# Attention over 32 small graphs on one core: the softmax shares spread by POOL and turned by PE, eight heads' weighted sums in one block, twelve places for turned tiles, one bank for values and output

## The reference

```python
q, k, v = (proj(Wq, bq), proj(Wk, bk), proj(Wv, bv))      # (b, 8, 256, 32) each
scores = jnp.einsum('bhqd,bhkd->bhqk', q, k) * SCALE       # SCALE = 32 ** -0.5
scores = scores * (adj + adj)[:, None, :, :]
attn = jax.nn.softmax(scores, axis=-1)
ctx = jnp.einsum('bhqk,bhkd->bhqd', attn, v)               # heads side by side: (b, 256, 256)
out = jnp.einsum('bse,fe->bsf', ctx, Wo) + bo
y = x + out
result = (y - mean(y)) / sqrt(var(y) + 1e-5)               # over the features
```

## Time and profile before

| | |
|---|---|
| median of three runs | 520.39 us (519.92 to 523.06) |
| the profiled execution, its own time | 522.89 us |
| its span, first to last instruction | 521.1 us |
| mean granted clock of TensorE | 0.974 of full |

### The profile page before, as it was taken

The page is one execution under the profiler, slowest core; times in us unless marked ns, Lnnn a source line. Parts: engine busy times, 40 slices in busy tenths (PEclk is TensorE's granted clock), DMA queues, the critical chain, the costliest instruction groups (busy, mean ns, idle before and its releaser), DMA issues.

```text
span 521.1 us, 15227 instructions
## 1 busy us (share of the span) xinstructions
PE 472.7 (91%) x4742; PEld 395.2 (76%) x4742; DVE 429.8 (82%) x1815; ACT 384.0 (74%) x1257; POOL 348.7 (67%) x518
## 2 busy tenths in 40 slices
PE   4569999999999999999999999999999999998872
PEld 3357887878788788878888787878888787877752
DVE  4547888888888898888888998988889888888881
ACT  2478887777878777787878777787878777777750
POOL 4724557686876767696876767786776768664444
PEclk9859999999999999999999999999999999999996
DMA  5709897988889798898889897998989889795101
GB/s 161 173 29 240 207 222 176 233 202 205 227 208 240 173 254 193 218 219 206 227 202 235 199 244 173 230 219 205 231 187 260 187 220 214 165 246 128 61 23 41
DMA packets 40322, 100.11 MB, mean 192 GB/s; under 512 B 9649, under 2 KB 17842, under 8 KB 40242
## 3 DMA queue, kind: packets, MB, share of 16 engines
q1 hardware_dynamic: 26930, 73.96, 60.8%
q10 hardware_dynamic: 13312, 25.17, 16.8%
HBM read 26.22 MB, written 8.39 MB: 66 GB/s over the span
## 4 chain that ended last, share of the span: by engine, by line
PE 65%; POOL 21%; issue 5%; DVE 4%; ACT 3%; DMA 1%; POOLq 0%; DVEq 0%; SPq 0%; ACTq 0%
PE turn_bank L223 17%; PE proj_bank L240 11%; PE v_bank L253 9%; PE row_bank L211 8%; PE ctx_bank L278 8%; POOL xt_parts L546 7%; PE ctx_bank L266 5%; PE out_bank L290 5%; POOL parts L540 4%; POOL result L586 3%; POOL ctx_parts L554 2%; POOL scale L573 2%; POOL parts L538 2%; ACT probs L447 2%; POOL ctx_parts L552 1%
## 5 line engine op out<-in xcount | busy, mean ns | idle before, releaser
L447 ACT ACTIVATE probs<-probs,low_top 128x256 f32<-128x256 f32 x512 | 257.6, 505 | 100.9 <-DVE low_top L349 98.4
L356 DVE COPY turned_probs<-turn_bank 128x512 f32<-128x512 f32 x224 | 154.7, 691 | 53.7 <-PE turn_bank L223 52.9
L341 DVE CUSTOM_DVE_ANT_0 probs<-row_bank,adj_rows 128x256 f32<-128x256 f32 x512 | 192.2, 414 | 6.1 <-PE row_bank L211 6.1
L223 PE MATMUL turn_bank<-ident,probs 128*128 128x128 f32 x1024 | 158.2, 277 | 7.8 <-ACT probs L447 7.7
L223 PEld LDWEIGHTS turn_bank<-ident,probs 128*128 128x128 f32 x1024 | 119.5, 141 | 52.1 <-ACT probs L447 23.4
L240 PE MATMUL proj_bank<-xt_parts,w_parts 128*128 128x512 f32 x360 | 107.0, 407 | 21.4 <-POOL xt_parts L546 16.2
L211 PE MATMUL row_bank<-stack 128*128 128x256 f32 x512 | 124.3, 325 | 0.7 <-DVE top L341 0.7
L447 ACT ACTIVATION_READ_ACCUMULATOR probs<-probs,low_top 128x1 f32 x512 | 97.3, 190 | 0.0
L540 POOL TENSOR_TENSOR parts<-whole,parts 128x512 fp32r<-128x512 f32 x64 | 82.9, 1296 | 5.3
L240 PEld LDWEIGHTS proj_bank<-xt_parts,w_parts 128*128 128x128 f32 x360 | 61.0, 193 | 30.8 <-POOL xt_parts L546 19.2
L552 POOL CAST ctx_parts<-context 128x256 fp32r<-128x256 f32 x64 | 25.5, 398 | 86.0 <-DVE context L366 86.0
(11 more groups left out here) (44 smaller groups left out, 473.0 us busy)
## 6 DMA issues: line engine op xcount, KB each, us to landing
stack<-parts SPq DMA_DIRECT2D x492, 128.0 KB, 2.6
xt<-in_x_t SPq DMA_DIRECT2D x16, 512.0 KB, 3.9
adj_rows<-in_adj ACTq DMA_DIRECT2D x16, 512.0 KB, 4.7
xr<-in_x ACTq DMA_DIRECT2D x16, 512.0 KB, 7.5
out<-result ACTq DMA_DIRECT2D x32, 256.0 KB, 3.2
turned_probs<-in_wk SPq DMA_DIRECT2D x1, 256.0 KB, 4.0
turned_probs<-in_wq SPq DMA_DIRECT2D x1, 256.0 KB, 3.8
turned_probs<-in_wv SPq DMA_DIRECT2D x1, 256.0 KB, 4.0
```

What stands on the lines that cost most here:

```text
L223: last = nc.tensor.transpose(turn_bank[o % 2][:, c * S + t * P:c * S + (t + 1) * P], probs[:, o % RING, t * S + c * P:t * S + (c + 1) * P] ...
L341: last = nc.vector.tensor_tensor_reduce(probs[:, o % RING, t * S:(t + 1) * S], row_bank[o % 2][:, t * S:(t + 1) * S], adj_rows[:, (n // 2) ...
L356: nc.vector.tensor_copy(turned_probs[:, o, :], turn_bank[o % 2][:]).then_inc(moved_dve, 1)
L447: last = nc.scalar.activation(tile, tile, ACT.Exp, bias=low_top[:, n % 2, o, t:t + 1], accum_out=sums[:, n % 2, o, t:t + 1])
```

## The change

The two halves of a graph are joined. DVE divides once for eight heads, at head 7 of step g, and `sums` and `shares` are laid out with the node tile outside and the head inside. A new instruction on POOL, `spread_shares`, at head 7 of step g, ahead of whatever else stands there and behind `add_bias`, copies the 16 shares of a partition, each repeated 32 times, into `wide` (128x512). PE's `turn_shares` is then four plain 128x128 transposes of `wide` into a bank of their own, `inv_bank`; it waits for POOL's copy. It and `weigh_v`, now 32 matmuls for eight heads into the whole of `ctx_bank`, stand at head 1 of step g+1; at head 5 nothing is left. ACT's `copy_inverse`, DVE's `scale_context` and POOL's `cut_context` handle 512 columns once in a graph, at heads 2, 3 and 3 of step g+1. `turned_probs` has 12 places used in turn in place of 8. To free the bank for `inv_bank`, values and output share one: `project_v` also waits until the residual of the graph two back has been read from it, `project_out` until ACT has copied the values of graph g+2. The two uses of the bank stand where they stood.

```diff
+TURNED = 12
...
-        sums = sb("sums", [P, 2, H, T])
-        shares = sb("shares", [P, 2, H, T])
+        sums = sb("sums", [P, 2, T, H])
+        shares = sb("shares", [P, 2, T, H])
         probs = sb("probs", [P, RING, T * S])
-        turned_probs = sb("turned_probs", [P, H, T * S])
-        inverse = sb("inverse", [P, S])
-        context = sb("context", [P, 2, S])
+        turned_probs = sb("turned_probs", [P, TURNED, T * S])
+        wide = sb("wide", [P, T, H, D])
+        inverse = sb("inverse", [P, 2 * S])
+        context = sb("context", [P, 2 * S])
...
-        w_whole = turned_probs[:, 4:8, :].rearrange("p w (t e) -> p w t e", t=T)
+        w_whole = turned_probs[:, 8:12, :].rearrange("p w (t e) -> p w t e", t=T)
...
+        inv_bank = bank("inv_bank")
...
-        v_bank = bank("v_bank")
+        v_bank = out_bank
...
             def project_v(n):
                 if n == 0:
                     pe.wait_ge(w_cut, 3)
+                    pe.wait_ge(bias_ready, 1)
+                wait(pe, y_ready, n - 2)
                 wait(pe, v_ready, n)
...
-            def turn_shares(g, half_):
-                pe.wait_ge(shares_ready, 2 * g + half_ + 1)
-                wait(pe, ctx_ready, 2 * g + half_)
-                for t in range(T):
-                    for o in range(J * half_, J * half_ + J):
-                        c = D * (o % J)
-                        nc.tensor.matmul(ctx_bank[c:c + D, S + t * P:S + (t + 1) * P],
-                                         shares[:, g % 2, o, t:t + 1].to_broadcast([P, D]), ident[:], start=True, stop=True,
-                                         tile_position=(0, c), skip_group_check=True)
-            def weigh_v(g, half_):
-                if half_ == 0:
-                    pe.wait_ge(v_ready, g + 1)
-                for o in (J * half_ + J - 1, *(n for n in ON_ACT if n // J == half_)):
+            def turn_shares(g):
+                pe.wait_ge(widened, g + 1)
+                wait(pe, inverted, g)
+                for half_ in range(2):
+                    for t in range(T):
+                        last = nc.tensor.transpose(inv_bank[:, half_ * S + t * P:half_ * S + (t + 1) * P],
+                                                   wide[:, t].rearrange("p h d -> p (h d)")[:, half_ * P:(half_ + 1) * P],
+                                                   ident[:])
+                last.then_inc(inv_made, 1)
+            def weigh_v(g):
+                pe.wait_ge(v_ready, g + 1)
+                wait(pe, ctx_ready, g)
+                for o in (H - 1, *ON_ACT):
                     wait_moved(pe, g, o)
-                for t in range(T):
-                    for o in range(J * half_, J * half_ + J):
-                        c = D * (o % J)
-                        last = nc.tensor.matmul(ctx_bank[c:c + D, 0:S], v[:, (g // 2) % 2, g % 2, t, o * D:(o + 1) * D],
-                                                turned_probs[:, o, t * S:(t + 1) * S], start=(t == 0), stop=(t == T - 1),
-                                                tile_position=(0, c), skip_group_check=True)
+                for half_ in range(2):
...
+                        for o in range(J * half_, J * half_ + J):
...
                 last.then_inc(ctx_made, 1)
...
             def project_out(g):
-                pe.wait_ge(ctx_low, 2 * g + 2)
-                wait(pe, y_ready, g)
+                pe.wait_ge(ctx_low, g + 1)
+                pe.wait_ge(v_ready, min(g + 3, B))
...
                     if o == 1 and is_graph(g - 1):
-                        turn_shares(g - 1, 1)
-                        weigh_v(g - 1, 1)
+                        turn_shares(g - 1)
+                        weigh_v(g - 1)
                     if o == 2 and is_graph(g + 1):
                         project_v(g + 1)
-                    if o == 5 and is_graph(g):
-                        turn_shares(g, 0)
-                        weigh_v(g, 0)
                     if o == 6 and is_graph(g - 1):
                         project_out(g - 1)
...
             def move_turned(g, o):
...
-                wait(dve, ctx_made, 2 * g - 1 + o // J)
-                nc.vector.tensor_copy(turned_probs[:, o, :], turn_bank[o % 2][:]).then_inc(moved_dve, 1)
-            def divide(g, half_):
-                dve.wait_ge(probs_ready, 8 * g + J * half_ + J)
-                heads = slice(J * half_, J * half_ + J)
-                nc.vector.reciprocal(shares[:, g % 2, heads, :], sums[:, g % 2, heads, :]).then_inc(shares_ready, 1)
-            def scale_context(g, half_):
-                dve.wait_ge(inverted, 2 * g + half_ + 1)
-                wait(dve, ctx_low, 2 * g + half_ - 1)
-                nc.vector.tensor_tensor(context[:, half_, :], ctx_bank[:, 0:S], inverse[:],
-                                        ALU.mult).then_inc(ctx_ready, 1)
+                wait(dve, ctx_made, (H * g + o - TURNED) // H + 1)
+                nc.vector.tensor_copy(turned_probs[:, (H * g + o) % TURNED, :], turn_bank[o % 2][:]).then_inc(moved_dve, 1)
+            def divide(g):
+                dve.wait_ge(probs_ready, H * g + H)
+                wait(dve, widened, g - 1)
+                nc.vector.reciprocal(shares[:, g % 2], sums[:, g % 2]).then_inc(shares_ready, 1)
+            def scale_context(g):
+                dve.wait_ge(ctx_made, g + 1)
+                dve.wait_ge(inverted, g + 1)
+                wait(dve, ctx_low, g)
+                nc.vector.tensor_tensor(context[:], ctx_bank[:], inverse[:], ALU.mult).then_inc(ctx_ready, 1)
...
-                        divide(g - 1, 1)
+                    if o == 7 and is_graph(g):
+                        divide(g)
...
                     if o == 3 and is_graph(g - 1):
-                        scale_context(g - 1, 1)
-                    if o == 4 and is_graph(g):
-                        divide(g, 0)
-                    if o == 6 and is_graph(g):
-                        scale_context(g, 0)
+                        scale_context(g - 1)
...
-                                                accum_out=sums[:, n % 2, o, t:t + 1])
...
             def move_turned(g, o):
...
-                wait(act, ctx_made, 2 * g - 1 + o // J)
-                if g == 0:
-                    act.wait_ge(bias_ready, 1)
-                nc.scalar.copy(turned_probs[:, o, :], turn_bank[o % 2][:]).then_inc(moved_act, 1)
-            def copy_inverse(g, half_):
-                act.wait_ge(ctx_made, 2 * g + half_ + 1)
-                wait(act, ctx_ready, 2 * g + half_)
-                nc.scalar.copy(inverse[:], ctx_bank[:, S:2 * S]).then_inc(inverted, 1)
+                wait(act, ctx_made, (H * g + o - TURNED) // H + 1)
+                nc.scalar.copy(turned_probs[:, (H * g + o) % TURNED, :], turn_bank[o % 2][:]).then_inc(moved_act, 1)
+            def copy_inverse(g):
+                act.wait_ge(inv_made, g + 1)
+                wait(act, ctx_ready, g)
+                nc.scalar.copy(inverse[:], inv_bank[:]).then_inc(inverted, 1)
...
                     if o == 2 and is_graph(g - 1):
-                        copy_inverse(g - 1, 1)
+                        copy_inverse(g - 1)
...
-                    if o == 6 and is_graph(g):
-                        copy_inverse(g, 0)
...
-            def cut_context(g, half_):
-                pool.wait_ge(ctx_ready, 2 * g + half_ + 1)
+            def spread_shares(g):
+                pool.wait_ge(shares_ready, g + 1)
+                wait(pool, inv_made, g)
+                nc.gpsimd.tensor_copy(wide[:].rearrange("p t h d -> p (t h) d"),
+                                      shares[:, g % 2].rearrange("p t h -> p (t h)").unsqueeze(2).to_broadcast([P, T * H, D])
+                                      ).then_inc(widened, 1)
+            def cut_context(g):
+                high, low = (ctx_parts[:, g % 2, n].rearrange("p f s -> p (f s)") for n in range(2))
+                pool.wait_ge(ctx_ready, g + 1)
                 wait(pool, out_made, g - 1)
-                nc.gpsimd.tensor_copy(ctx_parts[:, g % 2, 0, half_, :], context[:, half_, :]).then_inc(ctx_high, 1)
-                pool.wait_ge(ctx_high, 2 * g + half_ + 1)
-                nc.gpsimd.tensor_tensor(ctx_parts[:, g % 2, 1, half_, :], context[:, half_, :],
-                                        ctx_parts[:, g % 2, 0, half_, :].bitcast(F32), ALU.subtract).then_inc(ctx_low, 1)
+                nc.gpsimd.tensor_copy(high, context[:]).then_inc(ctx_high, 1)
+                pool.wait_ge(ctx_high, g + 1)
+                nc.gpsimd.tensor_tensor(low, context[:], high.bitcast(F32), ALU.subtract).then_inc(ctx_low, 1)
...
                 for o in range(H):
+                    if o == 7 and is_graph(g):
+                        spread_shares(g)
...
                     if o == 3 and is_graph(g - 1):
-                        cut_context(g - 1, 1)
+                        cut_context(g - 1)
...
                     if o == 6 and is_graph(g):
                         add_bias(g // 2, g % 2)
```

(23 more changed lines are left out.)

## The result

The changed kernel takes 583.47 us in the median of four runs (581.64 to 584.28), against 520.76 for the kernel before: a ratio of 1.120 (95% interval 1.118 to 1.122). The forecast was 571, 553 to 591, slower. The profiled execution took 581.64, with a span of 579.8 us; the other three took 583.45 to 584.28.

What follows compares the result with a forecast made beforehand. Not PE's 91% but a loop through DVE's context and POOL's queue was taken to bound the kernel. Longer pairs (+42.5) with start and end made +44, span 565; clock falls +7 made 572, or 571 as time; range 553 to 591.

Steps and rivals of the forecast that it cites:

- the loop: PE's head 3, DVE's context, POOL's queue, back to PE: sets the step; a pair 32.84 against 29.57 us.
- Odd: Odd step, head 3 to head 3: 2.05 to POOL's start, 8.55 POOL queue, 4.57 PE, 15.17 us in all.
- Even: Even step, head 3 to head 3: the odd step's sum plus two low_x on POOL, 2.50, making 17.67 us.
- PE's wait at low x: In even steps PE stands about 2.6 us until POOL has the low part of x ready.
- The spread: POOL's new 128x512 repeated-read copy: taken at 0.69 us with its wait, ends 0.40 and 1.30.
- The clock: PE's clock falls after the long wait in half of 13 even steps, 1.1 us each: +7, ends 0 and +20.
- Rival 1: PE's clock stays warm, all else as forecast: 564 us; chance 0.27.
- Rival 2: Spread dear (1.30 us) or PE cold in each even step: 578 to 590 us; chance 0.22.
- rival 3: PE is the bound and POOL's lag is made up, PE giving back 23.0 us: about 499; chance 0.06.
- Rival 4: Spread never late, only the even step's wait for low x grows: 521 to 545 us; chance 0.07.
- some 0.6 more: Odd steps: added PE time where heads 4 to 6 come faster than DVE and ACT make them, 0.6 us.
- places and bank: Twelve places for turned tiles and the bank shared by values and output: cost nothing.

Runs made afterwards that it cites:

- experiment 6: Changed kernel with DVE's scale_context and POOL's cut_context at head 2 in place of head 3: 528.02 us, ratio 1.013.
- experiment 10: Kernel before with only scale_context and cut_context of the second half at head 2 in place of head 3: 509.88 us, ratio 0.977.
- experiment 3: Changed kernel with 8 unread matmuls of 512 columns on PE just ahead of the wait for low x: 576.67 us, ratio 1.105.
- experiment 4: Changed kernel with 20 transposes of the identity on PE filling the wait for low x: 572.79 us.
- experiment 1: Changed kernel with POOL's spread moved ahead of add_bias: 555.44 us, ratio 1.066.
- experiment 7: Changed kernel with the context at head 2 and the spread ahead of add_bias: 526.49 us, ratio 1.009.
- experiment 11: Changed kernel with context at head 2, spread ahead of add_bias, and some key/query matmuls moved from head 4 to head 5: 513.09 us, ratio 0.985.
- experiment 5: Kernel before with only twelve places for turned tiles and one bank for values and output: 521.12 us, ratio 1.0005.
- experiment 2: Changed kernel with POOL's spread made twice, the extra copy into a spare tile: 589.96 us.
- experiment 9: Changed kernel without POOL's spread, PE laying the shares out as before with 32 matmuls on 32-column strips: 582.91 us.

## Why the prediction was right, and where it was off

- **What bounds the kernel.** Right. Not the 91% but the loop: the context's one-head shift (experiments 6 and 10) moved the time by 54 and 12 us with no work removed.
- **The sum of the steps.** Odd: 15.17 forecast, 15.24 measured. Even, clock at full speed: 17.67 forecast, 17.63 measured. PE's wait at low x was put at 2.6 and is 2.3; the wait for the spread at 1.0 and 0.4, measured 0.88 and, warm, 0.17 (in a cold step none). Thirteen pairs at full clock would be 42.9 above those of before, against 42.5. Outside the pairs the forecast had +2, for steps 0, 1 and 28, and nothing for all behind them. Measured is +2.1, in other places: nothing up to step 2's head 3, and all of it in the last steps, where the span ends 66.6 behind step 28's head 3 (513.23) and ended 64.5 before (456.61).
- **The spread.** Taken at 0.69 with its wait, measured 0.61 long and 0.62 from start to start: no dearer than the cast, the repeated read costs nothing.
- **The clock: the term that was mis-sized.** "A fall in half of the 13 even steps at 1.1: +7." Measured: a fall in 11 of 13 at 1.22, that is 13.4. The mechanism was right (experiments 3 and 4), its count was a guess between ends and came out near the far one. This is 6.4 of the 7.8 by which the span of 579.8 exceeds the 572 of the forecast. Of the other 1.4, 0.7 lies in the pairs (0.4 in their warm length, the rest in cold steps that are a little longer than 18.85) and the remainder is rounding. The ground "waits of 1.06 leave it at 1.00" holds for the rows that it names, but not in general: in experiment 3 the clock was at 0.50 behind waits of 1.05 and 0.96.
- **From the profiled run to the median.** The profiled execution is the fastest of the four, 1.8 under their median, while the profiled one of before was 2.5 above the median of three to which the forecast was scaled. The distance of 12.5 from 571 is thus 6.4 clock, 1.4 other terms and 4.7 the runs' scatter, to which the count of falls belongs.
- **Rival 1** (warm) had 564, a span of 565: by the pairs of experiment 3 the span would have been 566.8 here. **Rival 2** gave 578 to 590 and is what happened in its second form, the falls in nearly each even step. It had a chance of 0.22 where the forecast had 0.38. That the measured time still lies between 553 and 591 is owed to the far end of that range, which is this rival's, and not to the count of falls that the forecast took. **Rivals 3 and 4** are out: POOL's queue to the spread takes the 8.5 of its rows (295.37 to 303.89 in the odd step). Rival 4's sum is right for the case that it names, the spread ahead of add_bias: experiment 1 built it, and its pair is 17.24 + 14.15 where the sum has 17.23 + 14.17. But the ground on which rival 3 stood, PE's saving, holds in no version: it goes into waits for exponentials (experiments 7 and 11), which the prediction counted only as "some 0.6 more".
- **Nothing for places and bank**: right, by experiment 5.
- The Trainium skill (TensorE: Matmul & The Clock Gate, HAM oscillation) has a kernel go cold at every wait of its loop. The waits of that kernel were longer than the 2.3 here, and this trace does not quite follow it: the clock fell in 11 pairs of 13, and in 4 of 13 with the same wait in experiments 1 and 2. For the changed kernel the rule was nearer than the half I took; for those two it was further off.

What stays open: why a wait of 2.3 drops the clock in one pair and not in the next. Within one run it repeats: eleven times in a row here, every second or third pair in experiment 1, every third up to step 21 in experiment 2. The length of the pair alone does not settle it, as a pair is 32.9 warm and 34.1 cold here, 31.4 warm in experiment 1 and 34.0 warm in experiment 2. The place of the wait in time may matter; no run here varied that alone.

## What to carry to other kernels

Before taking work from the busiest engine, follow the last wait of a step around: if it closes a loop through another engine's queue, what counts is what that queue does between its late start and the instruction waited for. The average shares of both engines said nothing of it here. When halves are merged, each instruction gets cheaper per element, but the first result comes later and the longer instruction delays all that is queued behind it; look for a place where the consumer can take it one slot sooner, which here was worth 54 us and cost nothing. Leave work in each slot of the engine that feeds the others (experiment 11).

## What the runs showed of the hardware

- POOL's 128x512 copy with each of 16 values read 32 times took 0.608 us on average, as long as the plain cast of that size (0.618).
- The granted clock fell from 1.00 to 0.50 behind waits of 2.3 us of an otherwise loaded PE, in 11 of 13 pairs of the changed kernel, in 4 of 13 in experiments 1 and 2 and in 10 of 13 in experiment 9. In experiment 3 it was at 0.50 behind waits of 1.05 and 0.96, too.
- Within the wait of 2.3 us, 20 transposes (2.35 us) kept it at 1.00 in all 13 pairs, as did 8 matmuls of 512 columns (1.97 us).
- The 32 sums on 32-column strips took 1.87 us as one block, against 2 x 0.97 as two.
